# Position rows by transfer and a stacked table for the two smallest quads, in layer 0 of a two-layer graph kernel

## The chip, the cores and the metric

The kernel runs on one core of a Trainium2 chip. The metric is the device time of one execution in microseconds (us), taken as the median of three runs: 4264.1 us for the kernel before (4263.97 to 4264.62). Engines are named as in the profile: PE (TensorE), DVE (VectorE), ACT (ScalarE), POOL (GpSimd) and SP (SyncE, which here only starts transfers).

## The reference

Two layers of a graph network on 8192 nodes with 128 features and 262,144 edges, sorted by `dst`. Only layer 0 is touched by the change:

```python
def _L0_gnn_ref(x, edge_row, edge_col, edge_vals, W):
    gathered = x[edge_col] * edge_vals[:, None]
    pre_embed = jax.ops.segment_sum(gathered, edge_row, num_segments=N)
    return pre_embed @ W.T

x = layernorm(x + _L0_gnn_ref(x, src, dst, edge_weight, W))
x = layernorm(x + _L1_gnn_ref(x, [src, dst], edge_attr, w0, w1, w2, w3, w4))
```

For each edge, layer 0 fetches the feature row of node `dst`, scales it by the weight of the edge and adds it into the row of node `src`. The nodes are drawn so that `dst = 8192 * u**2` with u uniform: low-numbered nodes have many edges, so that sorted edges 0 to 8191 span 8 nodes, the next 8192 span 24, and so on.

## The kernel before, in words

**Layer 0** (`first_edges`). The edges lie as 128 rows of 2048, and each four rows form a *quad* (32 quads). First a sorting network on DVE and ACT orders the edges of each quad by `src`; then `transpose`s turn keys, weights and nodes into tables with one column per tile of 128 edges (`w_tab`, `id_tab`, `src_tab`). Then the main loop runs over 64 *parts* (16 tile numbers times 4 lanes; `hf`, `t`, `s`), and each part over 4 *groups* of 8 quads (`j`), 256 groups in all, numbered k. In a group, eight tiles of 128 edges are summed into the PSUM tile `l0_pre`. The feature rows of a tile come in one of two ways:

- *Gathered*: POOL starts an indirect DMA that reads 128 rows of `x` from HBM (L1092). This is done for 13 tiles of a part: 3 in each of the groups 0 to 2, and 4 in group 3 (`GATHERS`). Each lands in its own tile of `l_feat`. POOL may work up to 4 groups ahead of PE's sums (`AHEAD`, the wait on `summed`).
- *Picked*: for the other 19 tiles of a part (`PICKED`, 5, 5, 5 and 4 per group), whose nodes lie in a short span, the rows of that span are in SBUF from the start (`x_near`, three bf16 parts of each f32 value) and are picked by bf16 products with 0/1 matrices. The kind of a picked quad says how many blocks of 128 nodes it needs: S 1 block, D 2, U 3, T and M 2 and 1 blocks plus a rest of up to 42 nodes. A block costs 3 products (one for each bf16 part); a rest costs 1, since `x_rest` holds the three parts of its 42 nodes stacked in 126 partitions.

Each engine has its own program, and semaphores set the order. For picked tiles, a group k passes through these steps, each two or one groups ahead of the sums:

1. `spread` (PE, L1159): one bf16 product per picked tile copies the tile's row of node positions (`pos`) into all 128 partitions of the PSUM tile `place_b`.
2. `rest` (ACT, L800): copies `place_b` to `place` in SBUF, then two activations (L803, L807) make the 0/1 matrix of the third block or the rest. A single `place_b` serves all groups, so the next `spread` waits for this copy.
3. `near` (DVE, L987 and L988): two comparisons make the 0/1 matrices of blocks 0 and 1. They wait for the copy.
4. `fetch` (PE, L1179): the products, 23, 23, 27 and 21 in the four groups, into the PSUM tile `got`.
5. `message` (ACT, L815): copies `got` to `msg` in SBUF. A single `got` serves all groups.
6. `hots` (DVE, L997) makes the eight matrices that hold each edge's weight at its `src`; `sums` (PE, L1199) multiplies them with the rows, eight f32 products of 128x128 by 128x184. DVE adds `l0_pre` to `acc` once per part (L1008).

In PE's program a turn of the loop for group k is `spread(k + 2)`, `fetch(k + 1)`, `sums(k)`. Ahead of the loop, SP sends a table of offsets (`starts_i`) through HBM into one partition (`starts_row`, L712 and L714); DVE and PE wait for it before the loop.

**Behind the loop** a norm stage runs, and then layer 1, whose loop gathers 2048 tiles by indirect DMA (L1533). The change touches neither.

The wait that lets POOL run ahead, the order of PE's turn, and the start of the gathers:

```python
pool.wait_ge(summed, k + (SUMMED0 - AHEAD + 1))            # POOL, per group
...
spread(k + 2, later[1], later[0] * LH + later[2], later[3]) # PE, per group
fetch(k + 1, (j + 1) % GROUPS)
sums(k, part_no(wd, ws, hf, t, s), hf, t, s, j)
```

Of the kernel before, what the change touches and what calls it, by code (L numbers as in the profile page):

```python
# [36 lines left out]
P = 128  # L37
D = 128
# [17 lines left out]
PICKED = ((("S", 0, 1), ("S", 1, 2), ("D", 10, 4), ("T", 16, 5), ("M", 8, 7)),  # L56
# [13 lines left out]
BLOCKS = {"S": (0,), "M": (1,), "D": (0, 1), "T": (0, 1), "U": (0, 1, 2)}  # L70
RESTED = "MT"
ROOM = {"S": P, "M": P + REST, "D": 2 * P, "T": 2 * P + REST, "U": 3 * P}
SHIFT = {"M": P}
# [11 lines left out]
BLOCK_SLOTS = 32  # L85
# [5 lines left out]
SLOTS = 4  # L91

# [79 lines left out]
def gnn_kernel(nc, x, src, dst, attr, weight, w_lin, w_tp, consts, out, tables, x1):  # L172
# [10 lines left out]
    with ExitStack() as ctx:  # L183
        def sb(name, shape, dt):
            return ctx.enter_context(nc.sbuf_tensor(name, shape, dt))
# [3 lines left out]
        g.ident_bf = sb("ident_bf", [P, g.RN + 1], BF16)  # L189
# [43 lines left out]
def setup(nc, g, src, dst, weight, w_lin, w_tp, consts):  # L233

    RN, TN = g.RN, g.TN
    with ExitStack() as ctx:
# [35 lines left out]
        ident_made = sem("ident_made")  # L272
# [39 lines left out]
        def _(dve):  # L312
# [9 lines left out]
            nc.vector.tensor_copy(turn_bf[:], g.cst[:, C_TURN:C_TURN + P])  # L322
            nc.vector.tensor_copy(g.ident_bf[:, 0:RN], g.cst[:, C_IDENT:C_IDENT + RN])
            nc.vector.tensor_copy(g.ident_bf[:, RN:RN + 1], g.cst[:, C_IDENT:C_IDENT + 1]).then_inc(ident_made, 1)
# [74 lines left out]
        def _(pe):  # L399
# [15 lines left out]
            pe.wait_ge(ident_made, 1)  # L415
# [58 lines left out]
def first_edges(nc, g, x, stage):  # L474
# [11 lines left out]
    assert SHARES + 1 == 3 * BATCHES and len(BLOCK_LIST) <= BLOCK_SLOTS and len(REST_LIST) <= STAGED  # L486
# [16 lines left out]
    with ExitStack() as ctx:  # L503
# [20 lines left out]
        pos = sb("pos", [P, n], BF16)  # L524
        starts = sb("starts", [R, OFFS], F32)
# [10 lines left out]
        x_rest = sb("x_rest", [P, STAGED, D], BF16)  # L536
# [3 lines left out]
        place, rest_hot, rest_far = picks[4:6], picks[6:8], picks[8]  # L540
# [9 lines left out]
        lefts = [place_b[:, 0:BANK], got[:, 0:BANK], got[:, BANK:2 * BANK]]  # L550
# [35 lines left out]
        placed = sem("placed")  # L586
        copied = sem("copied")
# [25 lines left out]

        def columns(picked):
# [14 lines left out]

        def loaded(b, c, i):  # L630

            if share(b, c) is None:
                return 3, REST_LIST[i % len(REST_LIST)]
# [55 lines left out]
        def _(sp):  # L689
# [21 lines left out]
            spot = stage.rearrange("a b -> (a b)")[0:R * OFFS]  # L711
            sp.dma_start(spot.rearrange("(t v) -> t v", t=R), starts_i[:].bitcast(F32)).then_inc(starts_out, 16)  # L712
            sp.wait_ge(starts_out, 16)
            sp.dma_start(starts_row[0:1, :].bitcast(F32), spot.unsqueeze(0)).then_inc(starts_in, 16)  # L714

        @block.scalar
        def _(act):
            def split_step(b, i):
# [10 lines left out]
                else:  # L729
                    top = (P, 2 * REST, REST)[part]  # L730
                    to, rows = x_rest[0:top], rows[0:top]
# [62 lines left out]
            def rest(k, j):  # L794
# [8 lines left out]
                nc.scalar.activation(rest_far[:, cols], place[z][:, cols], ACT.Abs, bias=not_wanted[which - 2]  # L803
# [6 lines left out]
            def message(k, j):  # L810
# [4 lines left out]
                nc.scalar.copy(rows, got[:, 0:NF[j] * P]).then_inc(msg_made, 1)  # L815

            not_wanted = [turn_f[:, 7:8], turn_f[:, 4:5]]
            act.sem_inc(rest_made, 2)
            act.sem_inc(copied, 1)
            act.sem_inc(msg_made, 1)  # L820
            with act.Fori(0, n_turns) as wd:
                with act.Fori(0, n_src) as ws:
                    def slots(hf, t, last):
                        for s in range(LH):
                            for j in range(GROUPS):
                                k = group_no(wd, ws, hf, t, s, j)
                                h = part_no(wd, ws, hf, t, s)
                                if next_group(hf, t, s, j, 2, last):
                                    rest(k + 2, (j + 2) % GROUPS)
# [10 lines left out]
                    rest(k0, 0)  # L840
# [1030 lines left out]
```

## Time and profile before

| | |
|---|---|
| median of three runs | 4264.1 us |
| the profiled execution, whole / its span | 4263.51 / 4261.9 us |
| layer 0 up to the main loop | 0 to 508 us |
| layer 0 main loop (256 groups) | 508 to 1623 us |
| norm stage and the start of layer 1 | 1623 to 1700 us |
| layer 1 | 1700 to 4262 us |
| POOL, gathers of layer 0 / layer 1 | 832 / 2048, 946 to 947 ns each |

The profile is read by stretch: the share of an engine's busy time over the whole span mixes the sort, a PE stretch and a POOL stretch. Inside the loop, the waits say who is late, and the starts of one line's instructions give the period of a group. POOL's busy time leaves out about 0.3 us between two gathers that the views put down as "issue"; a period from start to start holds it.

### The profile page before, as it was taken

The numbers are of one execution on the slowest core, as the hardware profiler recorded it, in microseconds if no ns is written. First come the engines' busy times: TensorE is split into PE (matmuls) and PEld (weight loads), VectorE is DVE, ScalarE is ACT, GpSimd is POOL, SyncE is SP. The second block draws the span as 40 slices with busy tenths as digits, with TensorE's granted clock in tenths as the row PEclk, the third lists the DMA queues.
The fourth block names the chain that finished last, engine by engine and source line by source line (L and its number), as shares of the span: only waits on it lengthen the run. The fifth ranks groups of instructions, "written<-read, shape, count | busy, mean of one in ns | idle before, by whom it ended". The sixth has DMA issues, their size and how long they took to land.

```text
span 4261.9 us, 66445 instructions
## 1 busy us (share of the span) xinstructions
PE 2983.9 (70%) x19785; PEld 2619.5 (61%) x19786; DVE 2178.0 (51%) x4614; ACT 1136.9 (27%) x2095; POOL 2792.4 (66%) x2939
## 2 busy tenths in 40 slices
PE   2100399999999996776676776676666676676776
PEld 1000299999999995565555655565555555565665
DVE  8999877777777776323323323323323323323443
ACT  5444455555555554100100100100100100100211
POOL 5000177777777773777777777777777777777776
PEclk6555699999999996777777777777777777777777
DMA  1000111111111113222222222222222222222322
GB/s 57 0 0 20 52 51 49 49 49 49 51 49 49 49 49 102 56 56 56 56 56 56 56 56 56 56 56 57 56 56 57 56 56 56 56 56 61 87 81 63
DMA packets 109067, 228.22 MB, mean 54 GB/s; under 512 B 50674, under 2 KB 50818, under 8 KB 107858
## 3 DMA queue, kind: packets, MB, share of 16 engines
q0 software_dynamic: 93744, 194.44, 17.3%
q1 hardware_dynamic: 10658, 24.72, 1.8%
q10 hardware_dynamic: 4608, 8.39, 0.5%
q8 instruction: 27, 0.44, 0.0%
q14 instruction: 30, 0.24, 0.0%
HBM read 212.65 MB, written 8.40 MB: 52 GB/s over the span
## 4 chain that ended last, share of the span: by engine, by line
POOL 37%; issue 13%; PE 7%; DMA 2%; DVE 1%; POOLq 1%; ACT 0%; DVEq 0%; ACTq 0%
POOL feat L1533 37%; PE mixed L1663 3%; PE quad L1648 3%; DMA feat<-x,ids 2%; DVE group L1759 1%; PE attr_t L1614 1%; PE quad L1641 0%; POOLq L1526 0%; POOLq L1530 0%; POOLq L1529 0%; POOLq L1531 0%; ACT ids L1574 0%; DVEq L1759 0%; ACT z_last L1589 0%; PE y L1657 0%
## 5 line engine op out<-in xcount | busy, mean ns | idle before, releaser
L1533 POOL DMA_INDIRECT feat<-x,ids x2048 | 1937.5, 946 | 636.5 <-issue 621.0
L1092 POOL DMA_INDIRECT l_feat<-in_x,id_of x832 | 788.0, 947 | 726.6 <-issue 657.3
L1759 DVE TENSOR_TENSOR group<-group,quad 128x504 f32 (+1 forms) x512 | 348.1, 680 | 1723.6 <-PE quad L1648 1689.1
L1648 PE MATMUL quad<-attr_hot,feat 128*128 128x144 f32 x4096 | 809.6, 354 | 490.4 <-DMA feat<-x,ids 490.4
L1648 PEld LDWEIGHTS quad<-attr_hot,feat 128*128 128x128 f32 x4096 | 679.9, 235 | 631.1 <-DMA feat<-x,ids 380.1
L1663 PE MATMUL mixed<-group,mix 128*128 128x192 f32 x2304 | 678.5, 479 | 235.0 <-DVE group L1759 235.0
L1663 PEld LDWEIGHTS mixed<-group,mix 128*128 128x128 f32 x2304 | 637.6, 301 | 278.0 <-issue 247.0
L1574 ACT CAST ids<-src_col 128x8 int32 (+1 forms) x256 | 50.6, 197 | 2178.3 <-PE quad L1648 2178.3
L1738 DVE TENSOR_TENSOR attr_hot<-hot,attr_t 128x1152 f32<-128x1152 f32 x256 | 346.5, 1354 | 9.0
L1179 PE MATMUL got<-x_near,far_w 128*128 128x128 bf16 x5376 | 350.2, 220 | 1.2 <-DVE far_w L988 0.8
L997 DVE TENSOR_SCALAR w_row<-swap,src_of,w_of 128x184 f32<-128x184 f32 x1024 | 327.3, 389 | 0.1
L997 DVE TENSOR_SCALAR keys<-swap,src_of,w_of 128x184 f32<-128x184 f32 x1024 | 327.2, 389 | 0.0
L1179 PEld LDWEIGHTS got<-x_near,far_w 128*128 128x128 bf16 x5376 | 317.2, 98 | 1.7 <-issue 1.6
L800 ACT CAST far_w<-place_b 128x640 bf16<-128x640 f32 (+1 forms) x256 | 170.3, 665 | 486.5 <-PE place_b L1159 467.8
L1199 PE MATMUL l_pre<-keys,pad 128*128 128x184 f32 x1280 | 262.2, 319 | 0.0
L1199 PE MATMUL l_pre<-w_row,pad 128*128 128x184 f32 x1152 | 252.7, 319 | 0.0
L987 DVE TENSOR_SCALAR far_w<-far_w,cst 128x512 bf16<-128x512 bf16 (+1 forms) x256 | 94.4, 369 | 263.8 <-ACT far_w L800 261.2
L1199 PE MATMUL l_pre<-w_row,l_feat 128*128 128x184 f32 x896 | 225.4, 333 | 0.0
L1141 PE MATMUL l_pre<-cst,w_row 128*128 128x128 f32 x16 | 3.6, 404 | 305.5 <-DVE w_row L927 304.9
L1641 PE MATMUL quad<-zero_bf 1*128 1x504 bf16 x512 | 206.5, 403 | 12.1 <-issue 11.9
L1571 ACT ACTIVATE group<-group 128x1728 uint32<-128x1728 uint32 x128 | 210.2, 1642 | 13.0 <-issue 13.0
L1199 PEld LDWEIGHTS l_pre<-keys,pad 128*128 128x128 f32 x1280 | 212.7, 190 | 0.0
(258 smaller groups left out, 3198.5 us busy)
## 6 DMA issues: line engine op xcount, KB each, us to landing
feat<-x,ids POOLq DMA_INDIRECT x2048, 2.5
l_feat<-in_x,id_of POOLq DMA_INDIRECT x832
attr_in<-in_edge_attr SPq DMA_DIRECT2D x129, 72.0 KB
norm_x<-in_x SPq DMA_DIRECT2D x16, 256.0 KB, 2.7
x<-norm_z ACTq DMA_DIRECT2D x16, 256.0 KB, 2.4
x_t<-x SPq DMA_DIRECT2D x15, 256.0 KB, 3.2
out<-z_t ACTq DMA_DIRECT2D x15, 256.0 KB, 2.4
keys<-far_keys SPq DMA_DIRECT2D x2, 512.0 KB, 3.2
```

The source lines that it names most:

```text
L800: nc.scalar.copy(place[z][:, 0:used], place_b[:, 0:used]).then_inc(copied, 1)
L997: made = nc.vector.tensor_scalar(hot_of[(j % 2) * GROUP + i], iota[KIND[j][i]], src_of[s % 2][:, c:c + 1], w_of[s % 2][:, c:c + 1], ALU.is ...
L1092: pool.indirect_dma_start(feat[:, landing, :], None, x, bass.IndirectOffsetOnAxis(ap=id_of[s % 2][:, c:c + 1], axis=0)).then_inc(feat_in[l ...
L1179: last = nc.tensor.matmul(got[:, cols], hot, rows, start=(n_done == 0), stop=(n_done == len(products) - 1))
L1199: made = nc.tensor.matmul(pre[:, s % 2, bass.ds(places[i], WIN0)], rows, hot_of[(j % 2) * GROUP + i], start=False, stop=(j == GROUPS - 1 a ...
L1533: pool.indirect_dma_start(feat[z][:, t, :], None, x1, bass.IndirectOffsetOnAxis(ap=ids[z][h][:, t % H:t % H + 1], axis=0),).then_inc(feat_ ...
L1571: nc.scalar.memzero(group[z][:]).then_inc(group_zero, 1)
L1641: nc.tensor.matmul(quad[:, q, 0:NA * QUAD_WIN], zero_bf[0:1, 0:P], zero_bf[0:1, :], start=True, stop=False, skip_group_check=True)
L1648: last = nc.tensor.matmul(bank[:, :, bass.ds(places[t % H], WIN)], feat[z][:, t, :], attr_hot[h][:, t % H, :, :], start=False, stop=(t % Q ...
L1663: last = nc.tensor.matmul(mixed[:, 0:GROUP_WIN], g.mix[:, m, :], group[z][:, m, :], start=(m == 0), stop=(m == NA - 1))
L1738: nc.vector.tensor_tensor(attr_hot[h][:], hot[:].unsqueeze(2).to_broadcast(s4), by_tile[:, h * H:h * H + H, :].unsqueeze(3).to_broadcast(s ...
L1759: nc.vector.tensor_tensor(to, to, quad[:, q, 0:NA * QUAD_WIN].rearrange("p (m n) -> p m n", m=NA), ALU.add).then_inc(quad_added, 1)
```

## The change

Position rows no longer go through PE, PSUM and ACT. DVE makes `pos` a little earlier, SP writes the rows of the 19 picked quads to a table in HBM (19 transfers), and in the loop SP starts one transfer per part that reads one line of 4864 bytes (19 tiles of 128 bf16 positions) and lays it into all 128 partitions of `place`, which is double-buffered by part. `spread`, `place_b`, the copy L800 and `ident_bf` go. `near` and `rest` wait for the transfer at the first group of a part, and SP's transfer waits until `near` and `rest` are done with the buffer's last user, the part two before. `got` becomes two PSUM tiles, used in turn.

The two smallest quads get a new kind R: no block, only a rest of at most 42 nodes in `x_rest`, so one product in place of three. `x_rest` becomes two groups of four slots, `x_near` 28 slots in place of 32. Nothing else of the loop is changed: `GATHERS`, `hots` and the eight products of `sums` stay.

```diff
-PICKED = ((("S", 0, 1), ("S", 1, 2), ("D", 10, 4), ("T", 16, 5), ("M", 8, 7)),
-          (("S", 2, 1), ("S", 3, 2), ("D", 11, 4), ("T", 17, 5), ("M", 9, 7)),
+PICKED = ((("S", 2, 1), ("D", 10, 2), ("T", 16, 4), ("M", 8, 5), ("R", 0, 7)),
+          (("S", 3, 1), ("D", 11, 2), ("T", 17, 4), ("M", 9, 5), ("R", 1, 7)),
...
-BLOCKS = {"S": (0,), "M": (1,), "D": (0, 1), "T": (0, 1), "U": (0, 1, 2)}
+BLOCKS = {"R": (), "S": (0,), "M": (1,), "D": (0, 1), "T": (0, 1), "U": (0, 1, 2)}
...
+        place = [sb(f"place{z}", [P, len(PLACED) * P], BF16) for z in range(LH)]
-        place_b = ctx.enter_context(nc.psum_tensor("place_b", [P, 2 * BANK], F32))
-        got = ctx.enter_context(nc.psum_tensor("got", [P, 2 * BANK], F32))
+        got = [ctx.enter_context(nc.psum_tensor(f"got{z}", [P, 2 * BANK], F32)) for z in range(2)]
...
+        def wait_places(eng, wd, ws, hf, t, s, j):
+            if j == 0:
+                eng.wait_ge(placed[s % LH], (wd * PS + ws) * (HALVES * R * 16) + (hf * R + t) * 16 + 16)
...  (SP, ahead of the loop, between the waits for starts_made and the two starts transfers)
+            sp.wait_ge(pos_made, 1)
+            for m, c in enumerate(sorted(PLACED)):
+                own = pos[c * L:(c + 1) * L, :].bitcast(F32).rearrange("s (t e) -> s t e", e=words)
+                sp.dma_start(by_quad[m], own).then_inc(spread_out, 16)
...  (SP, after them)
+            sp.wait_ge(spread_out, 16 * len(PLACED))
+            by_part = spread.rearrange("(a f) -> a f", a=R * L)
+            with sp.Fori(0, n_turns) as wd:
+                with sp.Fori(0, n_src) as ws:
+                    for hf in range(HALVES):
+                        with sp.Fori(0, R) as t:
+                            for s in range(LH):
+                                k = group_no(wd, ws, hf, t, s, 0)
+                                sp.wait_ge(near_made, k + (NEAR0 - GROUPS))
+                                sp.wait_ge(rest_made, k + (NEAR0 - GROUPS))
+                                sp.dma_start(place[s][:].bitcast(F32),
+                                             by_part[bass.ds(t * L + (hf * LH + s), 1)].to_broadcast([P, len(PLACED) * words])
+                                             ).then_inc(placed[s], 16)
...  (ACT, rest)
-                act.wait_ge(placed, k + 1)
-                act.wait_ge(near_made, k + 1)
-                used = NF[j] * P
-                nc.scalar.copy(place[z][:, 0:used], place_b[:, 0:used]).then_inc(copied, 1)
-                act.wait_ge(copied, k + 2)
-                act.wait_ge(rest_made, k + 2)
+                act.wait_ge(rest_made, k + NEAR0)
...  (PE)
-            def spread(k, t, lane_s, j):
-                pe.wait_ge(copied, k + 1)
-                for m, i in enumerate(FETCHED[j]):
-                    v = (j * GROUP + i) * L + lane_s
-                    lane = g.ident_bf[:, v:v + 1].to_broadcast([P, P])
-                    last = nc.tensor.matmul(place_b[:, m * P:(m + 1) * P], lane, pos[:, bass.ds(t * P, P)], start=True,
-                                            stop=True)
-                last.then_inc(placed, 1)
...
-                pe.wait_ge(msg_made, k + 2)
+                pe.wait_ge(msg_made, k + 3)
...
-                                if later:
-                                    spread(k + 2, later[1], later[0] * LH + later[2], later[3])
```

On PE, a turn of the loop before, between the sums of a group and those of the next (here group 2 is fetched; `place_b<-pos` is `spread`, `got<-` is `fetch`, `l_pre<-` is `sums`, and the load reads the places for the sums):

```order
L1159 MATMUL place_b<-pos,ident_bf 128x128 x4
L1166 REGISTER_ALU
L1179 MATMUL got<-x_near,far_w 128x128 x24
L1179 MATMUL got<-x_near,far_keys 128x128 x3
L1207 ISA
L1207 TENSOR_LOAD starts_row
L1199 ISA
L1199 MATMUL l_pre<-w_row,l_feat 128x184
```

The same turn after (line numbers of the changed kernel):

```order
L1194 REGISTER_ALU
L1207 MATMUL got<-x_near,far_w 128x128 x24
L1207 MATMUL got<-x_near,far_keys 128x128 x3
L1235 ISA
L1235 TENSOR_LOAD starts_row
L1216 REGISTER_ALU
L1227 ISA
L1227 MATMUL l_pre<-w_row,l_feat 128x184
```

The spread is gone from PE's turn, and the rest stands in the same order. On SP, ahead of the loop and up to the next stage, before:

```order
L703 DMA far_w<-w_row 32x2048 x4
L706 DMA far_keys<-keys 64x2048 x2
L709 DMA far_w<-w_row 64x2048 x2
L712 DMA table<-starts_i 16x132
L714 DMA starts_row<-table 1x2112
L503 UNCONDITIONAL_BRANCH
```

And after, from the same transfers of `far_w` on to the loop (`table<-pos` are the 19 writes; the loads read the loop counts):

```order
L724 DMA far_w<-w_row 64x2048 x2
L734 DMA table<-pos 4x16x64 x19
L735 DMA table<-starts_i 16x132
L737 DMA starts_row<-table 1x2112
L600 TENSOR_LOAD n_pass
...
L746 ISA
L751 ISA
L751 DMA place<-table 128x1216
L749 REGISTER_ALU
```

The 19 writes stand ahead of the two transfers of the offsets for which DVE and PE wait, and a loop of 64 transfers follows.

## Rows read from the trace of the kernel before

**Rows 1.** By stretch: length, busy time (count) per engine, PE clock, DMA.
```profile
core 0: us, PE busy (x) PEld busy (x) DVE busy (x) ACT busy (x) POOL busy (x), PEclk, DMA share, GB/s
508.00:1623.00 1115.00, 1104.23 (x11323) 1052.00 (x11320) 847.75 (x2624) 588.53 (x1276) 787.96 (x832) 1.00 0.18 49
1700.00:4261.90 2561.90, 1784.67 (x8108) 1502.25 (x8106) 817.37 (x1346) 285.73 (x463) 1921.62 (x2035) 0.73 0.22 59
```

**Rows 2.** Waits inside the loop: waiting line <- releaser: us, times, longest.
```profile
ACT far_w L800 <- PE place_b L1159: 467.8, 243, 2.4
DVE far_w L987 <- ACT far_w L800: 261.2, 254, 1.8
POOL l_feat L1092 <- PE l_pre L1199: 68.0, 113, 0.9
```

**Rows 3.** Timeline of PE, one turn: start, us, line, tiles, count.
```profile
1008.35 0.44 PE L1159 MATMUL place_b<-pos,ident_bf 128*128 x5
1008.63 1.17 PE L1179 MATMUL got<-x_near,far_w 128*128 128x128 bf16 x18
1009.63 0.33 PE L1179 MATMUL got<-x_near,far_keys 128*128 128x128 bf16 x3
1009.93 0.57 PE L1199 MATMUL l_pre<-keys,l_feat 128*128 128x184 f32 x2
```

**Rows 4.** Timeline of PE at the loop's end, where no spread is left.
```profile
1616.02 1.17 PE L1179 MATMUL got<-x_near,far_w 128*128 128x128 bf16 x18
...
1617.22 0.57 PE L1199 MATMUL l_pre<-keys,l_feat 128*128 128x184 f32 x2
```

**Rows 5.** Timeline of PE: sums of the first and last group.
```profile
514.31 0.57 PE L1199 MATMUL l_pre<-keys,l_feat 128*128 128x184 f32 x2 [0.26 <-issue]
...
1619.81 0.47 PE L1199 MATMUL l_pre<-w_row,l_feat 128*128 128x184 f32 x2
...
1621.99 0.47 PE L1199 MATMUL l_pre<-w_row,pad 128*128 128x184 f32 x2
```

**Rows 6.** Timeline of POOL: first gather, and the 87th, ahead of its first longer wait.
```profile
508.35 0.94 POOL L1092 DMA_INDIRECT l_feat<-in_x,id_of  x1 [409.52 <-issue]
...
616.00 0.94 POOL L1092 DMA_INDIRECT l_feat<-in_x,id_of  x1 [0.30 <-issue]
```

**Rows 7.** Costliest lines, whole span: xcount | busy, mean ns | idle before, releaser.
```profile
L1533 POOL DMA_INDIRECT feat<-x,ids x2048 | 1937.5, 946 | 636.5 <-issue 621.0
...
L800 ACT CAST far_w<-place_b 128x640 bf16<-128x640 f32 (+1 forms) x256 | 170.3, 665 | 486.5 <-PE place_b L1159 467.8
```

**Rows 8.** Lines of the loop by shape, same columns.
```profile
L988 DVE TENSOR_SCALAR far_w<-far_w,cst 128x384 bf16<-128x384 bf16 x192 | 85.2, 444 | 0.0
L987 DVE TENSOR_SCALAR far_w<-far_w,cst 128x512 bf16<-128x512 bf16 x192 | 69.5, 362 | 191.8 <-ACT far_w L800 190.6 <-issue 1.3
L803 ACT ACTIVATE far_keys<-far_w,turn_f 128x256 bf16<-128x256 bf16 x128 | 65.0, 508 | 4.1
```

**Rows 9.** DMA issues: queue, xcount, KB each, median us to landing.
```profile
feat<-x,ids POOLq DMA_INDIRECT x2048, 2.5
...
keys<-far_keys SPq DMA_DIRECT2D x2, 512.0 KB, 3.2
w_row<-far_w SPq DMA_DIRECT2D x2, 512.0 KB, 4.5
...
table<-starts_i SPq DMA_DIRECT2D x1, 8.2 KB, 1.4
```

**Rows 10.** Timeline of SP ahead of the loop: start, time of the issues.
```profile
441.86 2.53 SPq L703 DMA_DIRECT2D far_w<-w_row  x4
...
496.81 0.32 SPq L712 DMA_DIRECT2D table<-starts_i  x1
```

**Rows 11.** Timeline of DVE: the first comparison of the loop.
```profile
508.26 0.41 DVE L987 TENSOR_SCALAR far_w<-far_w,cst 128x512 bf16<-128x512 bf16 x1 [0.97 <-ACT far_w L800]
```

**Rows 12.** Gathers of layer 0: duration ns min/median/max, first and last start.
```profile
L1092 POOL DMA_INDIRECT l_feat<-in_x,id_of x832: 938/944/1162, 508.4 to 1612.4; - x167
```

More of the change, by code:

```diff
@@ L84 @@
 REST_LIST = [c for c in sorted(PLACED) if PLACED[c] in RESTED]
-BLOCK_SLOTS = 32
+BLOCK_SLOTS = 28
+NEAR0 = 10
 WIN = 16
@@ L585, in first_edges @@
         feat_in = [sem(f"l_feat_in{i}") for i in range(RING)]
-        placed = sem("placed")
-        copied = sem("copied")
+        spread_out = sem("spread_out")
+        placed = [sem(f"placed{z}") for z in range(LH)]
         near_made = sem("near_made")
@@ L612, in holding, with placed_at @@
             return [m for m, i in enumerate(FETCHED[j]) if c in BLOCKS[PLACED[j * GROUP + i]]]
+        def wait_places(eng, wd, ws, hf, t, s, j):
+            if j == 0:
+                eng.wait_ge(placed[s % LH], (wd * PS + ws) * (HALVES * R * 16) + (hf * R + t) * 16 + 16)
+        def placed_at(s, j, cols):
+            first = sum(NF[0:j]) * P
+            return place[s % LH][:, first + cols.start:first + cols.stop]
         def columns(picked):
@@ L814, in message @@
                 rows = msg[j % 2].rearrange("p a b -> p (a b)")[:, 0:NF[j] * P]
-                nc.scalar.copy(rows, got[:, 0:NF[j] * P]).then_inc(msg_made, 1)
+                nc.scalar.copy(rows, got[j % 2][:, 0:NF[j] * P]).then_inc(msg_made, 1)
             not_wanted = [turn_f[:, 7:8], turn_f[:, 4:5]]
-            act.sem_inc(rest_made, 2)
-            act.sem_inc(copied, 1)
-            act.sem_inc(msg_made, 1)
+            act.sem_inc(rest_made, NEAR0)
+            act.sem_inc(msg_made, 2)
             with act.Fori(0, n_turns) as wd:
@@ L827, in slots @@
                                 h = part_no(wd, ws, hf, t, s)
-                                if next_group(hf, t, s, j, 2, last):
-                                    rest(k + 2, (j + 2) % GROUPS)
+                                ahead = next_group(hf, t, s, j, 2, last)
+                                if ahead:
+                                    wait_places(act, wd, ws, *ahead)
+                                    rest(k + 2, *ahead[2:])
                                 later = next_group(hf, t, s, j, GROUPS, last)
@@ L954, in _ @@
             dve.wait_ge(cols_cast, 2)
+            nc.vector.tensor_scalar(pos[:], dst_f, g.span_from[:, 1:2], None, ALU.subtract).then_inc(pos_made, 1)
             dve.wait_ge(miss_shown, 1)
             on = g.on[:, 1:2]
-            link(nc.vector.tensor_scalar(some[:], place_b[:, 0:2], 0.5, None, ALU.is_gt))
+            link(nc.vector.tensor_scalar(some[:], got[0][:, 0:2], 0.5, None, ALU.is_gt))
             link(nc.vector.tensor_reduce(wide[:], some[:], AX_X, ALU.max))
@@ L1027, in slots @@
                                 h = part_no(wd, ws, hf, t, s)
-                                if next_group(hf, t, s, j, 2, last):
-                                    near(k + 2, (j + 2) % GROUPS)
+                                ahead = next_group(hf, t, s, j, 2, last)
+                                if ahead:
+                                    wait_places(dve, wd, ws, *ahead)
+                                    near(k + 2, *ahead[2:])
                                 later = next_group(hf, t, s, j, 1, last)
@@ L1110, in keep_left @@
                 to = lefts[c].rearrange("p (a d) -> p a d", a=STAGED)
-                high = x_near[:, share(b, c), part, :] if share(b, c) else x_rest[:]
+                high = x_near[:, share(b, c), part, :] if share(b, c) else x_rest[:, rest_share(b, c)]
                 pe.wait_ge(split, 9 * b + i + 1)
@@ L1132, in _ @@
                     pe.wait_ge(cols_made, 1)
-                    nc.tensor.transpose(got[0:R, 0:P], first[:], ident).then_inc(first_turned, 1)
+                    nc.tensor.transpose(got[1][0:R, 0:P], first[:], ident).then_inc(first_turned, 1)
                 if b == 8:
@@ L1178, in fetch @@
                     for n_done, (hot, rows) in enumerate(products):
-                        last = nc.tensor.matmul(got[:, cols], hot, rows, start=(n_done == 0),
+                        last = nc.tensor.matmul(got[z][:, cols], hot, rows, start=(n_done == 0),
                                                 stop=(n_done == len(products) - 1))
```

76 lines of the change are left out of this document (40 added, 36 removed).

## The prediction

> **What bounds the kernel now.** I read the stretches first. In the main loop of layer 0, PE is busy for 1104 of 1115 us at the full 2.4 GHz clock (1.00), POOL for 788 and DVE for 848 [rows 1]; in layer 1 POOL is busy for 1922 of 2562 us. The change touches only the first of these. Then the waits inside it: ACT waits 468 us for the spread, DVE 261 us for ACT's copy, and POOL 68 us for PE's sums [rows 2]; PE has no wait of that size. So PE sets the pace, and the others wait for it, however long their sums look. In the timeline of PE I looked for gaps: spread, fetch and sums follow each other [rows 3]. The period of a group comes from the first sums of the loop (514.31) to the first of group 255 (1619.81): 1105.5 / 255 = 4.335 us, or 17.34 us for a part [rows 5].
>
> The question is what comes next when PE gets shorter. POOL's busy time (788) hides it, since it leaves out the 0.3 us between two gathers. Where POOL was not yet held by PE, its first 87 gathers started from 508.35 to 616.00: 107.65 / 86 = 1.252 us each [rows 6]. In layer 1, where POOL is the bound, it is (1937.5 + 621.0) / 2048 = 1.249 [rows 7]. A part has 13 gathers: 13 x 1.252 = 16.27 us, only 1.07 us below PE's 17.34. POOL is the second bound, close behind, and the change leaves its gathers alone.
>
> **The change, part by part.** *PE.* A spread of 5 products starts at 1008.35 and the fetch behind it at 1008.63; its first 18 products take until 1009.63: 0.056 us each either way [rows 3]. Per part 19 spread products go, and 2 fetch products in each of two groups, 23 in all: 23 x 0.0558 = 1.28 us. That these come off in full is shown at the loop's end, where no spread is left: from fetch to sums takes 1.20 us (1616.02 to 1617.22) against 1.30 with a spread ahead [rows 3, 4], so no gap opens. PE's part becomes 17.34 - 1.28 = 16.06 us, below POOL's 16.27.
>
> *ACT and DVE.* ACT loses 256 copies, 170 us [rows 7]; the third matrix of groups 0 and 1 grows from 256 to 384 columns, at most half of 508 ns more, 128 times, 33 us [rows 8]. DVE's first comparison in those groups shrinks. Both had room (589 and 848 of 1115 us) [rows 1] and the step that they waited for is gone. I cost these at nothing; the cover is that both work two groups ahead of the product that needs them. DVE at 13.2 us a part of work is also the next bound after POOL.
>
> *The second `got` tile and the moved waits.* PE's sums still need the copy of their own group; the fetch now needs one of two groups ago. PE showed no wait there, so this gains nothing and costs nothing.
>
> *The transfers in the loop.* The trace has no transfer of one line into 128 partitions, so I bound it. It moves 128 x 4864 bytes = 608 KB. Transfers of 512 KB on SP's queue landed in 3.2 and 4.5 us [rows 9]; scaled by 608/512 that is 3.8 to 5.3 us. I take 4.5, midway, as the two rows are of the same kind. It may start when the comparisons of the part two before are done, which DVE does two groups ahead; that leaves about five groups, 20 us, before its first use. The DMA engines are busy 18% [rows 1]; 64 transfers of 4.5 us add at most 288 us in 1041, so the queues stay half empty. A first cost of nothing, then, with 15 us of cover.
>
> *POOL's path.* 832 gathers from 508.35: the last starts at 508.35 + 831 x 1.252 = 1548.8. It lands 2.5 us later, as the gathers of layer 1 [rows 9], and two of the last group's eight products follow, 0.31 each [rows 5]: the loop's sums end at 1551.9. With layer 1's 1.249 it is 1549.4.
>
> *PE's path.* The loop starts later. SP is free at 496.81, when the offsets are made [rows 10]; `pos` is ready then. The 19 writes cost 0.32 us each by the single issue there, or 0.63 by the four in 2.53 us: 6.1 to 12.0 us of SP's time, with the two transfers for which PE and DVE wait behind them. The first lands after 1.4 us [rows 9], then comes the second, and at about 0.5 us later the first position transfer: 505 to 511, landing 3.8 to 5.3 us later, at 509 to 516.5. The first comparison stood at 508.26 [rows 11], so the loop's PE side starts 1 to 8 us later; I take 5. POOL's start doesn't hang on it: it needs tables that ACT makes, and runs 4 groups ahead. Its 14th gather, at 508.35 + 13 x 1.252 = 524.6, needs the first sums, which would end at 514.31 + 5 + 2.6 = 522: just in time. PE then needs 255 periods of 16.06 / 4 = 4.015: sums of group 255 start at 514.31 + 5 + 1023.8 = 1543.1 and end 2.65 us later (1621.99 + 0.47 - 1619.81) [rows 5], at 1545.8; with 8 us, 1548.8. This is below POOL's 1551.9 in either case.
>
> *Sum.* The sums ended at 1621.99 + 0.47 = 1622.46 [rows 5]. The new end is 1551.9: a gain of 70.6 us, of which I keep 70, since POOL and PE run so close that some wait must be left between them. What follows is not changed, and starts that much sooner. The profiled execution took 4263.51 us (span 4261.9 and 1.6 around it), the median is 4264.1, 0.6 more. 4263.5 - 70 = 4193.5, or 4194 on the median. PE's removed work alone would have given 64 x 1.28 = 82 us; POOL takes back 12 of them.
>
> **The rivals.** *A: the spread was cover.* PE's sequencer loads eight places ahead of each sums; with nothing in front of the fetch, that could stand in the open, and only the 256 removed fetch products would count: 256 x 0.0558 = 14 us, so 4250. Against it: the row at the loop's end without spread, where fetch to sums even shrank [rows 4]; for it, that this is one group out of 256.
>
> *B: POOL gets slower.* Gathers took 938 to 1162 ns, median 944 [rows 12]. If all that start during a position transfer took the longest (5.3 of 16.27 us, so 4.2 of 13 gathers, 64 times, 0.218 more each): 59 us back, a gain of 12, 4252. At half of that, 4223. Now that POOL is the bound, all that slows it counts, where before PE hid it. For it: two streams share the DMA engines for the first time in this loop. Against it: the transfer and the gather meet at the DMA engines, not in POOL's issue.
>
> The Trainium skill (SBUF — State Buffer, Who interferes with whom) says that GpSimd shares a pair of ports with VectorE, and that the later one is fully blocked while a VectorE instruction runs in a two-port mode, as comparisons like these may. By that rule each of the 512 comparisons could hold up POOL for its length, about 0.4 us [rows 8], 205 us in all, and on a POOL-bound loop this would turn the gain into a loss of some 130 us, 4392. The trace agrees only in part: comparisons of 384 columns, which take 444 ns in the mean, are slower than those of 512 (362), so it is DVE that waits; POOL's mean of 947 ns is 9 above its least (788 us for 832) [rows 1, 8, 12], 7 us in the whole loop and already in the 1.252.
>
> *C, on the other side: the position transfer is the bound.* If reading one line of HBM 128 times goes far slower than a copy of separate lines, each part waits for its transfer. Two are in flight by turns on one queue, so the loop's period becomes the time of one transfer. The change is slower than before from 17.34 us on, four times the rows' time; at 20 us a part, 64 x (20 - 17.34) = 170 us slower, 4434. Against it: the 512 KB transfers [rows 9] leave a factor of four.
>
> *D: it does not do what it says.* If 42 nodes did not hold a quad of kind R, the kernel would fall back to 135 passes, and the time would be many times the present. By the drawing of `dst` the two quads span 8 and 24 nodes; I leave it under 1 in 100.
>
> **How the numbers follow.** The forecast, POOL-bound at 16.2 to 16.6 us a part, gets 0.78: gains of 50 to 73 us, 4190 to 4214. A gets 0.06, B 0.10 (4214 to 4252), C (with the skill's rule in full, and D) 0.04, and 0.02 is left for a gain between 0 and 10 us. For an 8 in 10 range I go from 4188 (1.249 us a gather, the whole 73 us, and 2 us for runs) to 4224 (half of B). Above that lie A, most of B's other half, and C. About 0.2%, 8.5 us, is what a measurement of this kernel can tell from no change. Faster by more: forecast, A, B and a little of the rest, 0.95; within: 0.01; slower: 0.04.
>
> **What would show it.** In the changed profile: the loop's PE busy share falls below 99%, with waits of PE's sums for the DMA of `l_feat`, at the latest in the second half, as PE catches up by 0.2 us a part; POOL's wait for `l_pre` goes from 68 us to a few; the gathers start 1.25 us apart from the first to the last, the last at 1549; the position transfers land in 4 to 6 us, with no wait of DVE or ACT for `place` but the first; the norm stage starts near 1554. I would be wrong if PE stays without waits at a period above 4.07 us (A), if gathers last longer than 0.95 us (B), or if DVE or ACT waits for `place` in every part (C).

## The result, and the profile after

The changed kernel takes 4211.4 us (median of 4 runs, 4210.3 to 4212.1) against 4264.0 us for the kernel before (4 runs, 4262.5 to 4264.6). The ratio is 0.9877, with a 95% interval of 0.986 to 0.9894. That is 52.7 us less, where 70 were forecast: the time is inside the range of 4188 to 4224, 17 us above the forecast of 4194.

All of it lies in layer 0's loop. The stretches after, in the columns of [rows 1] (length, then busy time and count of PE, PEld, DVE, ACT and POOL, the clock, the DMA share, GB/s):

```profile
508.00:1570.00 1062.00, 1028.39 (x9856) 970.88 (x9856) 830.15 (x2628) 442.60 (x1021) 792.37 (x832) 0.99 0.30 89
1650.00:4208.00 2558.00, 1773.64 (x8101) 1493.62 (x8100) 816.98 (x1346) 285.60 (x463) 1919.94 (x2033) 0.74 0.22 59
```

PE is busy 76 us less than in [rows 1], but the loop is only 53 us shorter: PE's busy share fell from 99% to 97%. ACT lost 146 us, POOL gained 4. The clock is at the full 2.4 GHz in the loop, before and after. Next the timeline of PE after (start, us, line, tiles, count): the loop's first sums, one turn in the middle, and its last group.

```profile
519.73 0.53 PE L1227 MATMUL l_pre<-keys,l_feat 128*128 128x184 f32 x2
...
1003.97 1.17 PE L1207 MATMUL got<-x_near,far_w 128*128 128x128 bf16 x18
1004.97 0.33 PE L1207 MATMUL got<-x_near,far_keys 128*128 128x128 bf16 x3
1005.37 0.57 PE L1227 MATMUL l_pre<-keys,l_feat 128*128 128x184 f32 x2
...
1567.22 0.48 PE L1227 MATMUL l_pre<-w_row,l_feat 128*128 128x184 f32 x2
...
1569.40 0.47 PE L1227 MATMUL l_pre<-w_row,pad 128*128 128x184 f32 x2
```

The loop starts 5.4 us later than in [rows 5] and ends at 1569.87, 52.6 us sooner. A group takes (1567.22 - 519.73) / 255 = 4.108 us, 16.43 us for a part, where 16.06 was forecast for PE and 16.27 for POOL. The turn in the middle shows where it is: from the first of 21 fetch products to the sums it is 1.40 us, against 1.30 for the same 21 in [rows 3]. The 21 products take 21 x 0.0557 = 1.17, so TensorE now stands for 0.23 us ahead of the sums, where it stood for 0.13. Over all the loop's groups the median of that gap is 0.23 after and 0.14 before, except at the two turns of the loop bodies, where it is 0.47 and 0.31 against 0.41 and 0.22. About 0.1 us came on in each group.

The waits after, in the columns of [rows 2]:

```profile
ACT pad L849 <- PE got L1207: 482.0, 240, 3.3
DVE keys L1032 <- PE l_pre L1227: 126.4, 127, 1.3
DVE w_row L1032 <- PE l_pre L1227: 96.6, 127, 1.4
PEld l_pre L1227 <- issue: 67.3, 244, 0.5
POOL l_feat L1130 <- PE l_pre L1227: 28.0, 92, 0.3
DVE turn_f L1048 <- DMA starts_row<-table: 9.3, 1, 9.3
ACT far_keys L837 <- DMA place<-table: 6.8, 1, 6.8
```

ACT and DVE still wait for PE. POOL's row says less than it seems to: 28.0 us in 92 places is 0.3 us each, the usual time between two gathers, where before it was 68.0 us in 113 and up to 0.9. GpSimd is hardly held any more: its gathers (next rows) start (1560.9 - 508.4) / 831 = 1.267 us apart, 16.46 us for 13, beside PE's 16.43. But no wait of PE for a gather's DMA is in the list: PE is the pace, as before, only by little. The row that grew is the weight load of the sums, waiting for "issue", that is, for nothing that the profile shows: 67.3 us in 244 places, where the kernel before had this:

```profile
PEld l_pre L1199 <- issue: 23.8, 88, 0.4
```

ACT waits for a position transfer once, at the start, and never again.

The gathers after (as [rows 12]), and the two instructions of TensorE's sequencer that stand between the fetch and the sums:

```profile
L1130 POOL DMA_INDIRECT l_feat<-in_x,id_of x832: 938/944/1060, 508.4 to 1560.9; - x167
...
L1235 PEldq TENSOR_LOAD <-starts_row x256: 587/592/631, 518.0 to 1565.6; - x128
...
L1216 PEldq ALU_OP  x256: 32/32/36, 518.9 to 1566.2; - x128
```

The load of the eight starts took 592 ns in the median before as well. The register operation of L1216 has no counterpart in that place before: the order rows of the change show it behind the load, in the changed kernel alone. It makes the value that the sums wait for. Before, the sums' wait for `msg_made` had the same value (k + 2) as the wait of the fetch ahead of it; the change raised it to k + 3, which no other wait of the turn has.

The start, on SP and then on DVE:

```profile
496.91 8.13 SPq L734 DMA_DIRECT2D table<-pos  x19
505.08 0.34 SPq L735 DMA_DIRECT2D table<-starts_i  x1
506.91 0.24 SPq L737 DMA_DIRECT2D starts_row<-table  x1
509.51 29.32 SPq L751 DMA_DIRECT2D place<-table  x4
...
509.03 0.21 DVE L1048 TENSOR_SCALAR turn_f<-turn_f 128x1 f32<-128x1 f32 x1 [9.33 <-DMA starts_row<-table]
...
513.87 0.53 DVE L1022 TENSOR_SCALAR far_w<-place,cst 128x384 bf16<-128x384 bf16 x1 [3.67 <-DMA place<-table]
```

The 19 writes take 0.43 us each, and the first position transfer lands 4.36 us after its issue; the first comparison starts 5.6 us later than in [rows 11].

### The profile page after: what moved, and what is told of

Read it like the earlier page. It is cut to its first block, busy times and chain, and to the rows that moved or that the text cites. A ratio compares the mean times of both kernels' runs of the same rounds, so it can differ in the third digit from the quotient of the medians.

```text
span 4208.6 us, 63500 instructions
## 1 busy us (share of the span) xinstructions
PE 2897.8 (69%) x18313; PEld 2530.7 (60%) x18314; DVE 2159.1 (51%) x4612; ACT 990.2 (24%) x1839; POOL 2796.7 (66%) x2939
## 4 chain that ended last, share of the span: by engine, by line
POOL 36%; issue 13%; PE 8%; DMA 2%; DVE 1%; POOLq 1%; ACT 0%; DVEq 0%; ACTq 0%
POOL feat L1555 36%; PE mixed L1685 4%; PE quad L1670 3%; DMA feat<-x,ids 2%; DVE group L1781 1%; PE attr_t L1636 1%; PE quad L1663 0%; POOLq L1548 0%; POOLq L1552 0%; POOLq L1551 0%; POOLq L1553 0%; ACT ids L1596 0%; DVEq L1781 0%; PE y L1679 0%; ACT z_last L1611 0%
## 5 line engine op out<-in xcount | busy, mean ns | idle before, releaser
L1207 PE MATMUL got<-x_near,far_w 128*128 128x128 bf16 x4992 | 329.7, 220 | 10.2 <-DVE far_w L1023 10.2
L1207 PEld LDWEIGHTS got<-x_near,far_w 128*128 128x128 bf16 x4992 | 307.2, 98 | 25.3 <-issue 10.6
L849 ACT COPY pad<-got 128x640 f32<-128x640 f32 (+1 forms) x256 | 170.3, 665 | 497.6 <-PE got L1207 482.0
L1227 PE MATMUL l_pre<-keys,l_feat 128*128 128x184 f32 x768 | 195.0, 336 | 17.7 <-issue 10.6
```

Of the source, the lines that this page charges most:

```text
L849: nc.scalar.copy(rows, got[j % 2][:, 0:NF[j] * P]).then_inc(msg_made, 1)
L1207: last = nc.tensor.matmul(got[z][:, cols], hot, rows, start=(n_done == 0), stop=(n_done == len(products) - 1))
L1227: made = nc.tensor.matmul(pre[:, s % 2, bass.ds(places[i], WIN0)], rows, hot_of[(j % 2) * GROUP + i], start=False, stop=(j == GROUPS - 1 a ...
```

## The experiments

Theory 1: the register operation of L1216 stands in the open once per group, behind the load, and costs about 0.1 us, 25 us in the loop. Theory 2 is rival A: the spread's products covered the load. Theory 3: the position transfers slow the gathers or TensorE's loads.

| Run | us, median (range) | kernel before, run beside it | first sums | loop's end |
|---|---|---|---|---|
| before | 4264.0 | | 514.31 | 1622.46 |
| after | 4211.4 (4210.3 to 4212.1) | 4264.0 | 519.73 | 1569.87 |
| 1 counts shared | 4201.4 (4200.8 to 4202.5) | 4268.0 (4261.9 to 4269.3) | 519.15 | 1557.47 |
| 2 before, one operation more | 4287.5 (4286.2 to 4288.2) | 4268.0 | 515.18 | 1644.40 |
| 3 stacked table alone | 4253.6 (4247.7 to 4255.5) | 4268.0 | 514.05 | 1609.28 |
| 4 transfers alone | 4230.8 (4230.5 to 4231.1) | 4268.0 | 520.85 | 1586.34 |
| 5 load ahead | 4195.8 (4194.8 to 4196.6) | 4263.6 (4262.7 to 4264.9) | 519.17 | 1554.45 |
| 6 one gather less | 4185.0 (4184.0 to 4186.3) | 4263.6 | 520.63 | 1546.34 |
| 7 four writes | 4221.2 (4219.7 to 4221.9) | 4263.6 | 529.88 | 1580.69 |
| 9 more transfers | 4212.9 (4210.9 to 4213.5) | 4263.6 | 521.47 | 1572.58 |
| 10 start order | 4207.1 (4206.4 to 4208.4) | 4263.2 (4261.4 to 4265.5) | 516.16 | 1566.77 |
| 11 both and the start | 4194.9 (4193.3 to 4196.7) | 4263.2 | 514.76 | 1554.58 |
| 12 load ahead alone | 4195.4 (4194.7 to 4195.8) | 4263.2 | 518.92 | 1553.59 |
| 13 load ahead, one gather less | 4131.9 (4131.4 to 4132.7) | 4264.2 (4262.6 to 4264.8) | 519.14 | 1491.66 |

First sums and loop's end are from each run's profile. (There is no number 8.)

### 1: the operation taken away

```
-            act.sem_inc(msg_made, 2)
+            act.sem_inc(msg_made, NEAR0 + 1)
...
-                pe.wait_ge(msg_made, k + 1)
+                pe.wait_ge(msg_made, k + NEAR0)
...
-                pe.wait_ge(msg_made, k + 3)
+                pe.wait_ge(msg_made, k + (NEAR0 + 2))
```

(and the same for `hot_made`)

> The kernel after, with the start values of two semaphores raised (msg_made by 9, hot_made by 10) so that TensorE's waits for them in a group fall on the values k+10, k+11 and k+12 that its registers hold already: one register operation per group goes, the one that stands between the load of starts_row and the first product of the sums. Theory 1 (that operation stands in the open once per group): the gap that the sums leave ahead of their first product falls by about 0.1 us in each of 256 groups, TensorE's part goes from 16.43 us to about 16.06 us, below the gathers' 16.27 us, so the gathers are the pace: loop's end 1548 to 1554 us in place of 1570 us, time about 4195 us (4190 to 4200). Theory 2 (rival A of the prediction: the spread's products were cover for the load of the starts, and the gap is what is left without them): no change, 4211 us within 2 us. Theory 3 (the position transfers slow GpSimd's gathers or TensorE's loads): no change, 4211 us within 2 us.

Measured: 4201.4 us, 10 us less than after (14 less when each is set against the kernel before that was run beside it, which took 4 us longer here). The median gap ahead of the sums is 0.14 us again. Waits in the loop (POOL's 40 are again of the usual 0.3 us), and the gathers:

```profile
PEld l_pre L1228 <- issue: 36.2, 139, 0.9
POOL l_feat L1130 <- PE l_pre L1228: 12.2, 40, 0.3
```

```profile
L1130 POOL DMA_INDIRECT l_feat<-in_x,id_of x832: 942/947/1322, 507.9 to 1554.0; - x167
```

There is no spread here either, the load is where it was, and the transfers run: theories 2 and 3 asked for no change and fall. The gathers now start 1046.1 / 831 = 1.259 us apart; the time is 1 us above theory 1's range, since they were taken at 1.252.

### 2: the operation added to the kernel before

```
+            pe.sem_inc(hot_made, 30)
...
-                        pe.wait_ge(hot_made, k + 1)
+                        pe.wait_ge(hot_made, k + 31)
```

> The kernel before, with the start value of hot_made raised by 30, so that the wait of the sums' first product for it falls on a value that no register holds: one more register operation per group, between the load of starts_row and the first product of the sums; nothing else moves. Theory 1: 0.1 us in each of 256 groups, about 25 us more: 4289 us (4283 to 4295). Theories 2 and 3: the operation lies beside the load or the queue and costs nothing, 4264 us within 2 us.

Measured: 4287.5 us, 19.5 above the kernel before run beside it and 23.4 above the 4264.0 of the first row; the loop ends 21.9 us later. One turn, with the spread still ahead of the fetch:

```profile
1005.08 0.44 PE L1160 MATMUL place_b<-pos,ident_bf 128*128 x5
1005.36 1.17 PE L1180 MATMUL got<-x_near,far_w 128*128 128x128 bf16 x18
...
1006.87 0.57 PE L1200 MATMUL l_pre<-w_row,l_feat 128*128 128x184 f32 x2
```

This fetch of 23 products takes 1.51 us to its sums, 0.23 more than 23 x 0.0557; in the kernel before such a group's gap is 0.14. With one operation more and nothing else, a kernel with the spread gets the wider gap (median 0.23 in most groups). A group takes (1641.74 - 515.18) / 255 = 4.418 us against 4.335: 0.083 us for an operation that the profile shows as 32 ns. The Trainium skill (Perfetto Trace Analysis, Sequencer-only Instruction) says that of such an instruction the profile reports the execution alone, while fetch, decode and the push of its update lie outside. The trace agrees: what is paid is more than twice what is shown.

### 3 and 4: each half of the change

Experiment 3 gives the kernel before the new `PICKED`, `BLOCKS` and `x_rest`, and keeps the spread; experiment 4 gives the kernel after the old ones.

```
+PICKED = ((("S", 2, 1), ("D", 10, 2), ("T", 16, 4), ("M", 8, 5), ("R", 0, 7)),
+BLOCKS = {"R": (), "S": (0,), ...}
```

> The kernel before with the stacked table alone: the two smallest quads are picked by one product each in place of three, the positions are still spread by products. 4 products fewer in each of 64 parts at 0.0557 us: 14.3 us less, 4250 us (4247 to 4253) under every theory in which TensorE is the pace of the kernel before; a smaller gain would mean that another engine is close behind.

> The kernel after without the stacked table: the positions come by transfers, the two smallest quads are picked by three products each as before. Theory 1 and 2 (TensorE is the pace of the kernel after too): 4 products more in each of 64 parts at 0.0557 us, 4225.6 us (4222 to 4229). Rival (GpSimd's gathers are the pace of the kernel after): the products fit into what TensorE waits, 4211 to 4216 us.

Measured: 4253.6 us, 14.4 less than the kernel before run beside it, where 14.3 were expected; median gap 0.14. And 4230.8 us, 1.8 above the range given, where the kernel before beside it took 4 us longer too. Against the kernel before, the transfers alone gain 37.3 us, the whole change 52.7 (each against the kernel before run beside it), so the stacked table is worth 15.4 in the kernel after too. TensorE is the pace there: its products count in full.

### 5 and 12: the load ahead of the fetch

```
                                 k = group_no(wd, ws, hf, t, s, j)
+                                places = pe_places(t, hf * LH + s, j)
                                 if next_group(hf, t, s, j, 1, last):
                                     fetch(k + 1, (j + 1) % GROUPS)
```

Experiment 5 does this to experiment 1's kernel, experiment 12 to the kernel after with its waits as they are.

> Experiment 1's kernel, with the load of a group's eight starts issued ahead of the fetch's products in place of behind them. Theory 1, carried on (what is left of the gap, 0.13 us per group, is the load itself, which TensorE's sequencer reaches too late): ahead of the fetch the load runs while the sums before it are still queued, the gap closes, TensorE's part falls to about 15.6 us, and the gathers alone are the pace at 1.244 to 1.252 us each: last gather at 1543 to 1549 us, time 4188 to 4194 us. Rival (the sequencer isn't ahead there, since it stands at the fetch's waits): the load's 0.59 us stands in the open ahead of each fetch, about 120 to 150 us more than experiment 1, 4320 to 4350 us. Rival (experiment 1 is bound by the gathers alone already): no change, 4201 us within 2 us.

> The kernel after with the load of the starts ahead of the fetch, and its waits as they are, so that the extra register operation still runs once per group, behind the fetch's products but no longer behind a load. Theory 1 in its narrow form (what stood in the open is the chain of load and operation behind a drained queue): without the load in that place the operation is hidden too, gap 0, the gathers are the pace, 4195 us within 3 us, as experiment 5. If the operation costs its 0.1 us wherever it stands on TensorE's sequencer: about 25 us of TensorE's time more than experiment 5 has, of which its slack under the gathers takes some 15 to 20: 4200 to 4206 us.

Measured: 4195.8 and 4195.4 us. Of experiment 5, TensorE's timeline, with a fetch of 27 products:

```profile
1004.44 1.50 PE L1208 MATMUL got<-x_near,far_w 128*128 128x128 bf16 x24
1005.78 0.33 PE L1208 MATMUL got<-x_near,far_keys 128*128 128x128 bf16 x3
1005.95 0.53 PE L1227 MATMUL l_pre<-w_row,l_feat 128*128 128x184 f32 x2
...
1008.19 0.57 PE L1227 MATMUL l_pre<-w_row,l_feat 128*128 128x184 f32 x2 [0.15 <-DMA l_feat<-in_x,id_of]
```

and its gathers:

```profile
L1130 POOL DMA_INDIRECT l_feat<-in_x,id_of x832: 940/944/1055, 507.5 to 1550.9; - x167
```

From fetch to sums it is 1.51 us = 27 x 0.0557: the gap is 0.00, in the median of every group. The sums now wait for gathers:

```profile
PE l_pre L1227 <- DMA l_feat<-in_x,id_of: 15.0, 36, 1.2
```

These start (1550.9 - 507.5) / 831 = 1.2556 us apart, 16.32 us a part: GpSimd is the pace, at last, as the prediction had it. Experiment 5 came out 1.8 us above its range, which took the gathers at 1.252 at most.

Experiment 12 has the operation, 256 times, and the same time. The time alone couldn't tell what the operation costs, since TensorE has over 1 us a part to spare here (16.32 against the 15.21 of experiment 13). The gap tells it. The operation, and one turn with 27 products:

```profile
L1215 PEldq ALU_OP  x256: 32/32/32, 517.9 to 1549.4; - x128
...
1151.21 1.50 PE L1207 MATMUL got<-x_near,far_w 128*128 128x128 bf16 x24
1152.55 0.33 PE L1207 MATMUL got<-x_near,far_keys 128*128 128x128 bf16 x3
1152.72 0.53 PE L1226 MATMUL l_pre<-w_row,l_feat 128*128 128x184 f32 x2
```

It is 1.51 us again, and the median gap over all groups is 0.00: the operation costs nothing where it doesn't stand behind a load at the end of TensorE's queue. The gain of experiment 5 over experiment 1 is small since that was at the gathers' pace already: 67.8 and 66.6 us below the kernel before, each against the runs beside it.

### 6 and 13: one gather of 13 left out

```
+                                    if landing == RING - 1:
+                                        continue
```

> Experiment 1's kernel with one gather of each part's 13 left out (its quad's sums take the rows of the landing before it, so the values differ). GpSimd's part then is about 15.0 us, and TensorE is left as the only pace. Theory 1: TensorE's part without the operation is about 16.09 us (gaps of before, 0.71 us, 90 products of the fetches at 0.0557 us, four times 2.592 us of sums): loop's end about 1548 us, 4191 us (4188 to 4194). Rival (something else than the gathers, such as the position transfers, keeps experiment 1 at 4201 us): no change, 4201 us within 2 us.

> Experiment 5's kernel (load ahead of the fetch) with one gather of each part's 13 left out as in experiment 6 (values differ in the same way). If the load hidden took its 0.13 us per group, and 0.4 and 0.2 us at the loops' turns, off TensorE, and only the gathers kept that from the time in experiment 5: TensorE's part is 90 products at 0.0557 us and four times 2.55 us of sums, 15.2 us, GpSimd's 12 gathers at 1.2556 us are 15.07 us; loop's end about 1497 to 1503 us, the time 4136 to 4146 us. Rival (the gap only moved to another place on TensorE): no change against experiment 6, 4185 us within 3 us.

Measured: 4185.0 and 4131.9 us. TensorE's sums in experiment 6, first, first of the last group, last:

```profile
520.63 0.92 PE L1230 MATMUL l_pre<-keys,l_feat 128*128 128x184 f32 x2
...
1543.69 0.47 PE L1230 MATMUL l_pre<-w_row,l_feat 128*128 128x184 f32 x2
...
1545.87 0.47 PE L1230 MATMUL l_pre<-w_row,pad 128*128 128x184 f32 x2
```

and in experiment 13:

```profile
519.14 0.93 PE L1229 MATMUL l_pre<-keys,l_feat 128*128 128x184 f32 x2
...
1489.01 0.47 PE L1229 MATMUL l_pre<-w_row,l_feat 128*128 128x184 f32 x2
...
1491.19 0.47 PE L1229 MATMUL l_pre<-w_row,pad 128*128 128x184 f32 x2
```

In experiment 6 a group takes 1023.06 / 255 = 4.012 us, 16.05 a part: the 16.06 that the prediction worked out for TensorE, to 0.01. In experiment 13 it is 969.87 / 255 = 3.803, 15.21 a part. So the load behind the fetch costs TensorE 0.84 us a part, 54 us in the loop, which the gathers hide in experiment 5. Both times came out below the ranges given. In experiment 13 it is by 4 us, from a margin on the period that wasn't needed. In experiment 6 it is by 3 us: the loop's end was expected at 1548 and came at 1546.34, and the rest lies behind the loop and isn't explained.

### 7 and 10: the start

Experiment 7 writes the positions by lane, in 4 transfers; the quads that are picked are not neighbours, so the positions land under other quads and other rows are picked, with the same work. Experiment 10 makes `pos` before the run starts and puts the two transfers of the offsets among the 19 writes.

```
+            for v in range(L):
+                own = pos[v:L * len(PLACED):L, :]...
+                sp.dma_start(by_lane[v], own).then_inc(spread_out, 16)
```

```
+                if m == 9:
+                    sp.wait_ge(starts_made, 1)
+                    sp.dma_start(spot..., starts_i...).then_inc(starts_out, 16)
+                if m == 14:
+                    sp.wait_ge(starts_out, 16)
+                    sp.dma_start(starts_row...).then_inc(starts_in, 16)
```

> The kernel after with the positions written out by 4 transfers (one per lane, 19 partitions each) in place of 19: 15 issues of 0.43 us go from SyncE's queue ahead of the starts' two transfers, 6.4 us. Where the start-up delay is paid in full (TensorE is the pace): first sums 5 us earlier, at about 514.5 us, and the time 5 us less, 4206 us (4205 to 4208). Where the gathers were the pace from the start: no change, 4211 us.

> The kernel after, with the start in another order and nothing changed in the loop: VectorE makes the positions before the run starts, SyncE issues 9 of the 19 writes of positions, then the starts' write, 5 more, the starts' load, and the last 5. If the start-up delay of 5.4 us is paid in full by a kernel that TensorE paces: starts_row lands at about 502 us in place of 509, first sums at 514 to 515 us, the time 4.5 to 5.5 us less than after, 4206 to 4207 us. If the gathers paced the kernel after from its start: no change, 4211 us.

Experiment 7 missed: 4221.2 us, 9.8 more than after. Its SP:

```profile
496.79 13.05 SPq L734 DMA_DIRECT2D table<-pos  x4
509.88 4.36 SPq L735 DMA_DIRECT2D table<-starts_i  x1
516.88 0.25 SPq L737 DMA_DIRECT2D starts_row<-table  x1
```

Four writes took longer to issue than 19, and the write behind them 4.36 us in place of 0.34. It still tests the term, the other way round: the first sums come 10.2 us later and the time is 9.8 us longer. Experiment 10's SP:

```profile
493.36 3.84 SPq L739 DMA_DIRECT2D table<-pos  x9
497.24 0.33 SPq L734 DMA_DIRECT2D table<-starts_i  x1
...
499.74 0.28 SPq L737 DMA_DIRECT2D starts_row<-table  x1
500.06 1.77 SPq L739 DMA_DIRECT2D table<-pos  x5
506.07 12.70 SPq L753 DMA_DIRECT2D place<-table  x3
```

The offsets leave 7.2 us sooner, but the first position transfer only 3.4, and with it the first sums (516.16, 3.6 sooner, less than expected); the time is 4207.1, 4.2 less. In the kernel after, a microsecond at the start is a microsecond at the end.

### 11: all together

Experiment 5's kernel with the start of experiment 10.

> Experiment 5's kernel (no extra register operation, load ahead of the fetch) with the start in the order of experiment 10. If the gathers alone are its pace, at 1.25 us each from a first one at 508 us that the new order doesn't move: no change against experiment 5, 4195 us within 2 us. If TensorE still paced it: 5 us less, 4190 us.

Measured: 4194.9 us, the same as experiment 5, though the first sums are 4.4 us sooner: the gathers are the pace, and their start didn't come sooner. Experiments 5, 11 and 12 are the best of the kernels that do the whole work, 0.984 of the kernel before (0.9823 to 0.9856 for 11), 16 us faster than the change as it was made. Among the three there is no difference that can be told.

### 9: more transfers

```
+                                for to, v in ((extra[s], 768), (place[s][:].bitcast(F32), len(PLACED) * words)):
```

> The kernel after with a second transfer per part: 768 of the row's 1216 words once more, into all 128 partitions of a buffer that nobody reads, ahead of the one that is used. If the position transfers cost nothing in the loop (theory 1): 4211 us within 2 us. If they slow the gathers or TensorE's loads (theory 3), and by that make the 17 us that are missing from the forecast, 63 per cent of that again: about 4222 us; if the later landing is waited for, more still.

Measured: 4212.9 us. The DMA share from 520 to 1540 us rises from 0.30 to 0.37, so the transfers did run. The loop starts 1.7 us later, as the transfer that is used is issued second, and a group takes 4.112 us against 4.108. The added transfers cost next to nothing in the loop, and theory 3 falls a second time.

## Why the prediction was right or wrong

The time lies inside the range, but not for the reason forecast: POOL was to be the pace, and it was PE, at a period above the 4.07 us that the prediction itself had named as a sign of being wrong. The range reached up to 4224 to make room for half of rival B. B came to 4 us, and a cost that the prediction had at nothing filled the room. That part is luck.

**PE's part of 16.06 us, below POOL's 16.27: the step that failed.** The products were priced rightly: without the operation TensorE's part is 16.05 (experiment 6). What failed is "so no gap opens". It was read from one group at the loop's end [rows 4], whose gap is 0.03 us, while the turn in the middle [rows 3] has 0.13: there TensorE waits for its sequencer, so whatever is added to the sequencer at that point comes on in full. The change added one register operation there, 0.093 us a group, and the sentence that the rest stands in the same order overlooked it, though the rows of the order that stand ahead of it show it. Put into the prediction's own path for PE: 1545.8 + 0.4 for the later start + 255 x (4.108 - 4.015) = 1569.9, the measured end.

**POOL as the next bound: right, but not in this kernel.** 13 x 1.252 = 16.27 was forecast, 16.32 measured where the gathers do bind (experiment 5), with the time of 4195 to 4196 that goes with it. In the changed kernel TensorE stayed above it at 16.43, so 18 us of the gain in the loop were not had.

**The start: right.** 5 us were taken and 5.4 came; SP's writes took 8.1 us, within the 6.1 to 12.0 worked out. With POOL as the bound it would have cost nothing (experiment 11); with TensorE it was paid.

**The position transfers, ACT and DVE at nothing: right.** The first transfer lands in 4.36 us (3.8 to 5.3 forecast), nobody waits for one after the first, and 63% more of their bytes change next to nothing (experiment 9). ACT and DVE wait for PE.

**The rivals.** A's sign came true (a period above 4.07 us with PE as the pace), and its place, the sequencer's work ahead of the sums; its mechanism did not. The load stood in the open before the change as well, with the spread ahead of it (a median gap of 0.14 in the kernel before and in experiment 3), and it did so no more without the spread (0.14 in experiment 1). B: the gathers' mean went from 947 to 952 ns, 4 us in the loop. The Trainium skill's rule on the shared ports (SBUF — State Buffer, Who interferes with whom), by which the loop could have turned to a loss, isn't borne out either: the gathers' median stayed at 944 ns beside the comparisons. In which mode these run, no row shows. (The price of this rival was added wrongly: 4194 + 205 is 4399, not 4392.) The prediction's reading that VectorE waits in GpSimd's place stays open: it rested on comparisons of 384 columns being slower than those of 512, but in the changed kernel the second comparison of 384 columns takes 326 ns in the mean (444 before), less than the first one of 512 columns (384). C and D did not come.

## What to carry to other kernels

Where a timeline shows an engine standing for "issue" in every turn, its sequencer is the pace at that point: count every register operation and load between that point and the last full queue, before and after, and look at which waits share a value, since a new offset in a wait can be an instruction. Check "no gap opens" in the middle of the loop, and by the mean over all turns, not in the last one. Loads of addresses belong behind long queued work (here ahead of the fetch, behind the sums), where they cost nothing in these runs.

## What the runs showed of the hardware

- A register operation of 32 ns in the profile cost 0.083 us a group behind a load (experiment 2), and nothing where products were still queued (gap 0.00, experiment 12).
- A load of eight values into TensorE's registers takes 0.59 us; behind the fetch it cost 0.21 us a group ((16.05 - 15.21) / 4), and ahead of it the gap is 0.00.
- Four writes of 19 partitions took 3.3 us each to issue, 19 writes of 4 partitions 0.43 us each, for the same 304 KB in all (4 x 76 and 19 x 16). The Trainium skill (DMA: Bandwidth & Descriptors, Why a DMA increments its semaphore by 16 and not by 1) says that a transfer runs on the largest number of engines up to 16 that divides the slowest dimension of both sides: 1 engine for 19, 4 for 4. The DMA share during the writes (the figure before the last, of 16 engines) agrees with that order, 16 x 0.08 = 1.3 engines' time for the four writes and 16 x 0.23 = 3.7 for the 19, though no row here names the engines. The first row is of experiment 7, the second of the kernel after:

```profile
498.00:510.00 12.00, 3.90 (x16) 3.00 (x16) 1.58 (x1) 3.74 (x12) 1.31 (x2) 0.54 0.08 18
498.00:505.00 7.00, 3.72 (x16) 3.01 (x16) 1.71 (x1) 1.98 (x6) 0.00 (x0) 0.58 0.23 37
```

- One line of 4864 bytes read into 128 partitions, 608 KB, lands in 4.36 us, within what copies of separate lines took when scaled to its size (3.8 to 5.3, from [rows 9]), and with the loop's DMA share at 0.30 the gathers' mean went from 947 to 952 ns.
